# Top-k in two steps per five groups of products, pieces of it on GpSimd and ScalarE, and a scaling two heads later

## The reference, cut to what matters

```python
mod = (silu(c) @ wmod).reshape(8, 6, 1, 256); sa, ca, ga, sb, cb, gb = ...
h = layernorm(x) * (1 + ca) + sa                       # x: 8 batches x 512 tokens x 256
x = x + ga * attention(h)                              # 16 heads, causal, latent keys and values
h = layernorm(x) * (1 + cb) + sb                       # 4096 tokens
scores = sigmoid(h @ gate_w.T)                         # 4096 x 16 experts
topk_score, topk_ids = top_k(scores.T, 512)            # each expert takes its 512 best tokens
xin = h[topk_ids]
eo = silu(xin @ gw + gb) * (xin @ up_w + up_b)         # F = 1024
eo = eo @ down_w + down_b
out = zeros.at[topk_ids].add(eo * topk_score)
shared = (silu(h @ sh_gate_w.T) * (h @ sh_up_w.T)) @ sh_down_w.T   # 512 wide, all tokens
x = x + gb * (out + shared)
```

## Time and profile before

| | us |
|---|---|
| median of 3 runs | 1139.32 (1138.76 to 1142.98) |
| profiled execution, its own time | 1144.72 |
| span of the profiled execution | 1142.9 |
| TensorE busy | 1103.9 (97%) |
| VectorE busy | 873.1 (76%) |
| GpSimd busy | 675.3 (59%) |
| ScalarE busy | 594.3 (52%) |

### The profile page before, as it was taken

How to read it: one execution, slowest core, us unless ns; L and a number is a source line. 1 busy time by engine, 2 the same in 40 slices (tenths; PEclk the granted TensorE clock), 3 DMA queues, 4 the chain that set the end, 5 groups by cost and what they waited for, 6 DMA issues and landing times.

```text
span 1142.9 us, 20775 instructions
## 1 busy us (share of the span) xinstructions
PE 1103.9 (97%) x6970; PEld 836.1 (73%) x6970; DVE 873.1 (76%) x2173; ACT 594.3 (52%) x1085; POOL 675.3 (59%) x771
## 2 busy tenths in 40 slices
PE   9899999999999999999899999999999999999996
PEld 4655656656656568888878888888888888888885
DVE  5677888888887687878887788777887777887662
ACT  2357777877876663222254444544445534455441
POOL 5234586687676554443866656566565656566544
PEclk9589999999999999999999999999999999999999
DMA  6435457766867553866345554555545565445621
GB/s 203 85 80 126 112 135 179 177 146 183 188 133 172 201 179 111 271 216 172 99 147 160 136 133 123 162 135 138 140 120 157 135 156 132 118 149 135 171 56 19
DMA packets 100329, 165.37 MB, mean 145 GB/s; under 512 B 18424, under 2 KB 65016, under 8 KB 98176
## 3 DMA queue, kind: packets, MB, share of 16 engines
q1 hardware_dynamic: 83600, 137.44, 42.8%
q0 software_dynamic: 14336, 25.70, 11.8%
q10 hardware_dynamic: 2288, 0.92, 0.6%
HBM read 103.71 MB, written 34.11 MB: 121 GB/s over the span
## 4 chain that ended last, share of the span: by engine, by line
PE 62%; issue 9%; POOL 9%; DVE 8%; DMA 5%; ACT 4%; SPq 1%; ACTq 1%; POOLq 0%; DVEq 0%
PE LB L587 14%; PE MB L587 13%; PE LB L973 5%; PE MB L973 5%; PE UB L587 4%; PE LB L679 4%; PE UB L717 4%; DMA XL<-xD 2%; PE MB L974 2%; PE LB L974 2%; PE XB L587 2%; DVE junk L1382 2%; PE MB L656 2%; POOL HTl L2019 1%; POOL EO L2031 1%
## 5 line engine op out<-in xcount | busy, mean ns | idle before, releaser
L2019 POOL TENSOR_TENSOR HTl<-HF,HTh 128x512 fp32r<-128x512 f32 x156 | 217.3, 1399 | 129.5 <-ACT HTh L1132 126.4
L1382 DVE CUSTOM_DVE_ANT_0 junk<-MB,MK 128x256 bf16<-128x256 f32 (+3 forms) x512 | 220.1, 486 | 56.8 <-PE MB L656 56.0
L1900 POOL TENSOR_SCALAR_AFFINE_SELECT P<-P 128x256 f32<-128x256 f32 x256 | 99.4, 411 | 122.9 <-ACT P L1071 122.4
L2087 POOL DMA_INDIRECT out_y<-EO,IDX x64 | 100.8, 1575 | 86.1 <-DVE EO L1854 72.9
L1143 ACT ACTIVATE SIL<-LB,gbT 128x512 f32<-128x512 f32 x64 | 43.8, 684 | 185.0 <-PE LB L587 185.0
L656 PE MATMUL MB<-KS,QS 48*128 48x256 f32 (+3 forms) x512 | 130.0, 365 | 4.8 <-DVE NM L1382 2.9
L1069 ACT ACTIVATE P<-LB 128x768 f32<-128x768 f32 x128 | 103.7, 810 | 57.8 <-PE LB L679 57.8
L1132 ACT ACTIVATE HTh<-HF 128x512 fp32r<-128x512 f32 x156 | 97.7, 627 | 65.0 <-DVE HF L1737 64.9
L679 PE MATMUL LB<-QS,KS 50*128 50x256 f32 (+3 forms) x512 | 123.1, 355 | 8.6 <-ACT P L1069 5.7
L679 PEld LDWEIGHTS LB<-QS,KS 50*128 50x128 f32 x512 | 77.7, 188 | 56.1 <-issue 31.0
L1737 DVE SCALAR_TENSOR_TENSOR HF<-MB,ubT,SIL 128x512 f32<-128x512 f32 x64 | 47.7, 745 | 62.9 <-PE MB L587 28.0
(11 more groups left out here) (326 smaller groups left out, 2947.4 us busy)
## 6 DMA issues: line engine op xcount, KB each, us to landing
WR<-in_gw SPq DMA_DIRECT2D x16, 1024.0 KB, 8.0
WR<-in_uw SPq DMA_DIRECT2D x16, 1024.0 KB, 5.0
WR<-in_dw SPq DMA_DIRECT2D x16, 1024.0 KB, 5.2
QS<-ST SPq DMA_DIRECT2D x96, 128.0 KB, 3.7
KS<-ST SPq DMA_DIRECT2D x93, 128.0 KB, 4.5
hD<-h SPq DMA_DIRECT2D x8, 1024.0 KB, 7.3
XT<-hD SPq DMA_DIRECT2D x7, 1024.0 KB, 8.0
X<-in_x SPq DMA_DIRECT2D x8, 512.0 KB, 4.4
```

Of the source, the lines that this page charges most:

```text
L1382: m = e.tensor_tensor_reduce(junk[:, o:o + w], MB[:, o:o + w], MK[:, 512 - w:512], 1.0, -3e38, ALU.add, ALU.max, NM[:, k // 4, 4 * (k % 4) ...
L1900: m = e.affine_select(out=dd, in_=dd, compare_op=ALU.is_ge, fill=0.0, base=0, pattern=[[0, 2], [1, 128]], channel_multiplier=-1)
L2019: e.tensor_tensor(HTl[:, slot, :], hf_of(n)[:], HTh[:, slot, :].bitcast(F32), ALU.subtract).then_inc(g_ht, 1)
L2087: e.indirect_dma_start(out=out2, out_offset=bass.IndirectOffsetOnAxis(ap=IDX[x_ % 3][:, q:q + 1], axis=0), in_=EO[:, q, :], in_offset=None ...
```

## The change

- Steps of the top-k come at ticks `(5 * t + 1) // 2`, that is after two and three ticks in turn, where before it was every third. The last step thus comes at tick 103, not 123, and `W_INDEX` goes from 42 to 36.
- TensorE turns the scores (`UB<-C,S`) after its first count product, not at a tick of their own; ScalarE copies the result to `PT` at w = 13, not VectorE.
- GpSimd clears `SC` at w = 17 and makes the four low parts of expert 0's gate weights (`WG0l`); both were VectorE's.
- Expert 0's up weights are cut at w = 38 to 41 (before 42 to 45), and the one-hot matrix of expert 1 is built at w = 41, 43, 45 and 47 (before 43, 45, 47 and in expert 0).
- In attention the second half of `scale2` runs in head 6, not 4.

```diff
-W_CUTS = (18, 20, 22, 24, 42, 43, 44, 45)
-W_INDEX = 42
+W_CUTS = (18, 20, 22, 24, 38, 39, 40, 41)
+W_INDEX = 36
+def tick_of(t):
+    return (5 * t + 1) // 2
+STEP_AT = {tick_of(t): t for t in range(T_VAL2 + 2)}
...
         def topk_step(t):
-            if t == 0:
-                e.wait_ge(d_top, 1)
-                for k in range(4):
-                    m = e.transpose(UB[:, k * 128:(k + 1) * 128], S[:, k * 128:(k + 1) * 128], ident)
-                m.then_inc(p_top, 1)
-            elif T_BIT <= t < T_SEL - 1:
+            if T_BIT <= t < T_SEL - 1:
                 e.wait_ge(d_top, t + 1)
                 e.matmul(XB[:, 0:1], Gm, cnt, start=True, stop=True).then_inc(p_top, 1)
+                if t == T_BIT:
+                    for k in range(4):
+                        m = e.transpose(UB[:, k * 128:(k + 1) * 128], S[:, k * 128:(k + 1) * 128], ident)
+                    m.then_inc(p_spread, 1)
...
         def tick():
             ticks[0] += 1
-            if ticks[0] > 0 and ticks[0] % 3 == 0:
-                topk_step(ticks[0] // 3 - 1)
+            if ticks[0] > 0 and ticks[0] in STEP_AT:
+                topk_step(STEP_AT[ticks[0]] - 1)
...
-                    if k in (3, 4) and old2:
-                        scale2(b - 2, k - 3)
+                    if k in (3, 6) and old2:
+                        scale2(b - 2, k // 6)
...
+            if w == W_TOPK + 2:
+                e.wait_ge(p_spread, 1)
+                e.activation(PT[:], UB[:], ACT.Copy).then_inc(a_spread, 1)
...
-                if t == T_SPREAD:
-                    e.wait_ge(p_top, 1)
-                    e.tensor_copy(PT[:], UB[:]).then_inc(d_spread, 1)
                 if t == T_ZERO:
                     e.tensor_copy(iotab[:], iotaf)
-                    kept(e.memset(SC[:], 0.0))
...
-            if ticks[0] > 3 and ticks[0] % 3 == 0:
-                topk_step(ticks[0] // 3)
+            if ticks[0] > tick_of(T_BIT) and ticks[0] in STEP_AT:
+                topk_step(STEP_AT[ticks[0]])
...
-            if w in W_CUTS:
-                j = W_CUTS.index(w)
-                if j < 4:
-                    cut(e, piece_g(0), j)
-            if w in (43, 45, 47):
-                onehot(1, (w - 43) // 2)
+            if w in (41, 43, 45, 47):
+                onehot(1, (w - 41) // 2)
...
-            if w in (44, 45):
-                cut(w - 44)
-        cut(2)
-        cut(3)
+            if w == W_CUTS[0] - 1:
+                e.memset(SC[:], 0.0).then_inc(g_zero, 1)
+            if w in W_CUTS[:4]:
+                cut(piece_g(0), W_CUTS.index(w))
+            if w in (40, 42, 43):
+                cut(piece_u(0), (40, 42, 43).index(w))
+        cut(piece_u(0), 3)
```

More of the change, by code:

```diff
@@ L31 @@
 T_BIT = 1
-T_SPREAD = T_BIT + 3
 T_ZERO = T_BIT + 6
@@ L234, in block_program @@
         "p_mod", "p_fold", "p_rows", "p_hT", "p_qk", "p_v", "p_mx", "p_mt", "p_mm", "p_pv", "p_out", "p_h2T", "p_sc"))
-    p_gate, p_up, p_down, p_top, p_idx, p_turn = (sem(n) for n in ("p_gate", "p_up", "p_down", "p_top", "p_idx", "p_turn"))
+    p_gate, p_up, p_down, p_top, p_spread, p_idx, p_turn = (sem(n) for n in (
+        "p_gate", "p_up", "p_down", "p_top", "p_spread", "p_idx", "p_turn"))
     (a_s, a_rows, a_xh, a_hf, a_st, a_v, a_nm, a_p, a_us, a_hn, a_th, a_h2) = (sem(n) for n in (
@@ L239, in block_program @@
     a_sil, a_ht, a_cut, a_xt, a_score = (sem(n) for n in ("a_sil", "a_ht", "a_cut", "a_xt", "a_score"))
-    a_sd, a_sc6, a_w = (sem(n) for n in ("a_sd", "a_sc6", "a_w"))
+    a_sd, a_sc6, a_w, a_spread = (sem(n) for n in ("a_sd", "a_sc6", "a_w", "a_spread"))
     (d_s, d_w, d_modT, d_mod, d_mv1, d_hh, d_st, d_mx, d_rec, d_tf, d_mv2, d_h2, d_lg) = (sem(n) for n in (
@@ L247, in block_program @@
     d_warm = sem("d_warm")
-    d_hf, d_cut, d_tb, d_eo, d_top, d_oh, d_idx, d_xt, d_spread, d_raw = (sem(n) for n in (
-        "d_hf", "d_cut", "d_tb", "d_eo", "d_top", "d_oh", "d_idx", "d_xt", "d_spread", "d_raw"))
+    d_hf, d_cut, d_tb, d_eo, d_top, d_oh, d_idx, d_xt, d_raw = (sem(n) for n in (
+        "d_hf", "d_cut", "d_tb", "d_eo", "d_top", "d_oh", "d_idx", "d_xt", "d_raw"))
     (g_ks, g_fill, g_rs1, g_P, g_nf, g_hn, g_x2, g_rs2, g_h2, g_ht) = (sem(n) for n in (
@@ L253, in block_program @@
     g_sd, g_nm, g_w = sem("g_sd"), sem("g_nm"), sem("g_w")
-    g_cut, g_eo = sem("g_cut"), sem("g_eo")
+    g_cut, g_eo, g_zero = sem("g_cut"), sem("g_eo"), sem("g_zero")
     g_own = sem("g_own")
@@ L288, in n_low @@
     def n_low(p, j=3):
-        return n_cut(p, j) if p < 3 else 8 + 4 * (p - 4) + j + 1
+        return j + 1 if p == 0 else 4 + 4 * (p - 4) + j + 1
     def n_eo(e, q):
@@ L502, in load_piece @@
         def load_piece(p, src):
-            if p - 2 == piece_u(0):
-                e.wait_ge(g_cut, 4)
+            if p - 2 < 4:
+                e.wait_ge(g_cut, 4 * (p - 3))
             else:
@@ L541, in sync_program @@
             if w == 15:
-                e.wait_ge(d_spread, 1)
+                e.wait_ge(a_spread, 1)
                 for k in range(4):
@@ L987, in tensor_program @@
                     else:
-                        e.wait_ge(d_cut, n_low(piece_g(0)))
-                        e.wait_ge(g_cut, 2 + m_ // 2)
+                        e.wait_ge(g_cut, 6 + m_ // 2)
                 if x_ and m_ < 2:
@@ L1609, in topk_step @@
                 if n < 29:
-                    e.wait_ge(p_top, t - T_BIT + 1)
+                    e.wait_ge(p_top, t - T_BIT)
                     kept(e.tensor_scalar(drop, XB[:, 0:1], float(CAP), float(1 << (n + 1)), ALU.is_lt, ALU.mult))
@@ L1633, in topk_step @@
                 settled()
+                e.wait_ge(g_zero, 1)
                 e.wait_ge(c_sco, 64)
@@ L1636, in topk_step @@
             elif t == T_TIE:
-                e.wait_ge(p_top, T_SEL - T_BIT + 1)
+                e.wait_ge(p_top, T_SEL - T_BIT)
                 e.tensor_scalar(need, XB[:, 1:2], -1.0, float(CAP), ALU.mult, ALU.add)
@@ L1648, in topk_step @@
             elif t == T_POS:
-                e.wait_ge(p_top, T_SEL - T_BIT + 2)
+                e.wait_ge(p_top, T_SEL - T_BIT + 1)
                 kept(e.tensor_copy(offs, XB[:, 3:4]))
@@ L1653, in topk_step @@
             elif t == T_VAL:
-                e.wait_ge(p_top, T_SEL - T_BIT + 3)
+                e.wait_ge(p_top, T_SEL - T_BIT + 2)
                 kept(e.tensor_scalar(PT[:], UB[:], -1.0, None, ALU.add))
@@ L1819, in vector_program @@
                 glu(n_eglu(x_, m_) - 1, m_, ubT[:, x_, m_:m_ + 1])
-                if x_ == 0 and m_ == 0:
-                    onehot(1, 3)
                 if m_ < 4:
@@ L2031, in add, with cut @@
                 e.tensor_tensor(EO[:, q, :], tb[q % 2][:], XL[:, q, :], ALU.add).then_inc(g_eo, 1)
[L2033 to L2037, removed]
+        def cut(p, j):
+            (wh, wl), rv, ks, cs = cut_of(p, j)
+            if p == piece_u(0):
+                e.wait_ge(d_top, N_ALL)
+            e.wait_ge(a_cut, n_cut(p, j))
             e.tensor_tensor(wl[:, ks, cs], rv[:, ks, cs], wh[:, ks, cs].bitcast(F32), ALU.subtract).then_inc(g_cut, 1)
```

## The result

The changed kernel takes 1152.2 us (median of four runs, 1151.2 to 1153.7) where the kernel before takes 1139.0 beside it: a ratio of 1.0096, 95% interval 1.0077 to 1.0115. That is 11 us slower by the ratio (9 to 13), 13 by the medians. Forecast were 1146.2 us, with 1137 to 1152 as the range: the sign was right, and the time lies at the range's upper end (1150.2 by the ratio, 1152.2 by the median), near rival 3, for a reason that no rival named.

The account below looks back on a forecast made before the run. TensorE, busy 97% of the span, was taken as the bound, so only its waits or low clock could be won. Terms -0.7 + 1.7 + 5.9 - 1.3 + 0 + 1.3 = +6.9 on 1139.3 gave 1146.2 us, range 1137 to 1152.

Parts of the forecast that it names:

- rival 3: GpSimd becomes the trouble: its four pieces meet most short two-tick intervals, clock falls twice; +14 us, 1153.3 us, chance 0.12.
- Attention: Later second scaling: the 0.66 us wait in four blocks is not won, each ends 0.17 later; +1.3 us, bounds -2.6 and +2.5.
- Now follow what is late next: Attention step tracing the later scaling through head 7's exponentials, GpSimd's mask and `NMl` to ScalarE; 0.17 us later per block.
- The start: Top-k up to the bits: the count still waits for `GBt` until 459.0, TensorE one tick further; -0.7 us, bounds -1.4 and 0.
- The bits: Two-tick top-k steps: some meet GpSimd or an `HF`, most old waits go; +1.7 us, bounds -1.0 and +6.
- 5 of 13 short intervals are hit: Step in the bits term: at the earlier share of slowed steps, 5 x 0.5 = 2.5 us are lost.
- The end: Last count product to index product: VectorE needs about 21.5 us against TensorE's 15.4, so TensorE waits; +5.9 us.
- Behind the index: After the index product: the 2.9 us `tb` wait shrinks to a remainder of 1.6; -1.3 us, bounds -2.5 and 0.
- rival 2: Faster, VectorE quick where GpSimd leaves it alone: index wait 3.3 us, later wait goes whole; -6.6, 1132.7 us, chance 0.08.
- The clock: TensorE's low clock: one fall at the index product replaces the one after the 2.9 us wait; 0, bounds -1.7 and +1.7.
- the chances: Chance of slower by more than 5.7 us: three quarters of the forecast's own 0.53 plus rival 3, given as 0.55.

Follow-up runs that it names:

- only_scale: Kernel before with only the second scaling moved to head 6; ratio 1.0069 to the kernel before, attention 191.4 us.
- free_x: Kernel before with second scaling in head 6, its last two row groups read from another tile so the load of `X` need not wait; ratio 0.9992.
- two_rows: Kernel before with small pieces moved, second scaling in head 5, and a second `GBt` buffer so batch 1's row loads early; ratio 0.9932, 1132.9 us.
- end_44: Kernel before with small pieces moved, two-tick steps for the bits, then six ticks a step, index product where it stood before; ratio 1.0008.
- scale_back: Whole change with only the later scaling undone (heads 3 and 4, as before); ratio 1.0030 to the kernel before.
- pieces_back: Whole change with the old scaling, and the four weight pieces and clearing of `SC` back on VectorE; ratio 1.0049 to the kernel before.
- end_28: Whole change with the old scaling, two-tick steps for the bits only, index product 28 ticks behind the last count product; ratio 1.0016 to the kernel before.
- mix35_v4: Kernel before with small pieces moved, second scaling in head 5, other experts' values in four steps of four instructions; ratio 1.0012.

## Why the prediction was right in sign and short in size

- **Attention, +1.3 forecast, 7.9 us by only_scale (4.8 to 10.9).** This is the step that failed: "Now follow what is late next". It followed ScalarE and GpSimd, and free_x bears out the size that it got there, but a scaling that moves also moves the release of its input. The load of `X` stands in SyncE's queue with six kinds of transfers behind it, and the earlier trace rows show none of that queue. The bound of +2.5 for this term was drawn from the chain that was looked at, not from the queues left out. What the runs show in its place: SyncE held for `th` for 17.0 us where it was 4.9, and 5.6 us more in attention, all of it gone when the load is freed (free_x, 0.9992).
- **The start, -0.7.** The mechanism holds: in six traces with one buffer this count product stands 7.2 to 7.6 us behind the issue of the load (before 451.81 and 459.03, after 452.56 and 459.87), one tick further in the program as forecast, and two_rows, which loads the row early, wins 5 us. But the time is not fixed: the execution after entered the stage 1.9 us later (the last `shifts` of attention stand at 403.34 and 405.26), the load 0.8, so some 1.1 us were won ahead of it, which the term put at nothing: -1.8 in all.
- **The bits, +1.7.** Some 1 us too high; the step "5 of 13 short intervals are hit" is nearly borne out. Behind 465 us four of twelve are stretched, and the twelve together take 1.9 us more than twelve times 1.60; the thirteenth (459.87) lies in part in the low clock. What was put too low is what the three-tick steps lost before: their 27 intervals took 2.8 us more than 2.28 each, where the term took back only the 0.98 of the earlier trace rows, and the twelve that are left behind 465 us take 1.4. So about +0.6 is left when the clock is counted apart, an estimate from the two timelines. end_44 gives 0.9 us by the ratio (-0.7 to 2.5), less what its end costs (0.7 for `OH`).
- **The end, +5.9.** Right in its mechanism, 0.9 short. Waits of 5.26 (forecast 4 to 5), 1.39 (1 to 2) and 0.35 us, less 0.25 of before: +6.8. From the last count product VectorE was busy for 21.50 us, and 22.9 passed to the end of `OH` (forecast 21.5); TensorE had 16.0 us of work (15.4).
- **Behind the index, -1.3.** The wait for `tb` went whole (-2.9, beyond the bound of -2.5 given here, though rival 2 counted it), and the gather's wait grew from 0.7 to 1.2: -2.4.
- **The clock, 0.** Too low, and beyond its bound of +1.7. Behind the index product TensorE is busy for 5.57 us at 0.57 from 536 to 544 us, 2.4 us lost, where 1.7 were lost behind the wait for `tb`: +0.7. The other fall (461 to 465 us, 4 us at 0.57) loses 1.7 us. Before, the same fall lay at 449 to 453 us, ahead of a wait that the load of `GBt` set, and so could cost nothing: +1.7.
- **The sum.** From the traces the top-k's terms come to some 5.6 us (-1.8 + 0.6 + 6.8 - 2.4 + 2.4), as much as was forecast, by errors that cancel; scale_back has 3.4 us by its ratio (1.1 to 5.6). With 7.9 for the scaling in place of 1.3 the forecast's own sum would have been 1152.8; that this is so near the measured 1152.2 is luck in part, since the two runs that take the change apart add up to 0.99%, 11.3 us, and the forecast's terms to 13.5.
- **A slip in the chances.** Three quarters of 0.53 and rival 3 make 0.52, not 0.55; nothing else hangs on it.
- **Rival 3** gave the right time by a wrong cause: with GpSimd's pieces taken back (pieces_back) the kernel is not faster. The port rule named beside it (the Trainium skill, SBUF — State Buffer, "SBUF: two separate sides") is visible in single instructions, below, but the moved pieces were not what cost.

## What to carry to other kernels

When an instruction is moved, ask what its end releases, not only who reads its output: here the loss was a load of a later input, held at the head of SyncE's queue, and everything issued behind it. A wait for a small row loaded just in time (`GBt`, 128 KB) cost some 5 us, more than any reordering of the stage behind it gave here, and a kilobyte of buffer in each partition removed it. Where two engines had little idle time over a stretch (end_28, mix35_v4), moving the due times mostly renamed the wait; look for a wait on a transfer first.

## What the runs showed that was not expected

VectorE can stand for several instructions of GpSimd in a row. end_28, timelines of both:

```profile
548.92 1.30 POOL L2040 TENSOR_TENSOR WU0l<-WR,WU0h 128x512 fp32r<-128x512 f32 x1
549.71 5.33 DVE L1718 TENSOR_TENSOR OH<-R,iotab 128x1024 bf16<-128x1024 bf16 x1
550.18 2.52 POOL L2020 TENSOR_TENSOR HTl<-HF,HTh 128x512 fp32r<-128x512 f32 x2
552.67 1.29 POOL L2040 TENSOR_TENSOR WU0l<-WR,WU0h 128x512 fp32r<-128x512 f32 x1
```

This piece of `OH`, 1.25 us when nothing is in its way, starts while the first of GpSimd's four instructions runs and ends 1.1 us after the last of them; those keep their 1.3 us each. Where `OH` starts first it is the other way round, in the same trace:

```profile
559.55 1.25 DVE L1718 TENSOR_TENSOR OH<-R,iotab 128x1024 bf16<-128x1024 bf16 x1
559.68 2.24 POOL L2020 TENSOR_TENSOR HTl<-HF,HTh 128x512 fp32r<-128x512 f32 x1
```

By the Trainium skill (SBUF — State Buffer, "SBUF: two separate sides"), of a VectorE instruction with two SBUF inputs and a GpSimd instruction that reads SBUF, whoever starts first has the shared ports for its whole instruction. The rows agree, and add that the loser can stand for all of four instructions of the other in a row.
